# Row elimination on the Gram matrix in place of Gram-Schmidt, and unpadded keys for the first four maxima of each block

## The chip, the cores and the metric

The kernel runs on one core of a Trainium2 chip. The metric is the device time of one execution in microseconds. The engines are TensorE (PE, with its weight loads as PEld), VectorE (DVE), ScalarE (ACT), GpSimd (POOL) and SyncE (SP). Each takes its own instructions in program order and waits on semaphores. ACTq and SPq in rows are the two engines' queues as they issue transfers.

## The reference

Input x is [2, 512, 144] in float32, with a condition vector of 144 for each of the two batch rows. Three transformer layers and a rotation follow:

```python
x = layer0(x, c)   # attention with 16 heads of 9, then a mixture of 4 experts, top 2
x = layer1(x, c)   # attention with layer-normed q and k, then an MLP of 576
x = layer2(x, c)   # attention, then an MLP of 576
# the rotation
U, _ = jnp.linalg.qr(P)              # P is [144, 64]
R = expm(A)                          # A skew, 64 x 64, from silu(c) @ W.T + b
z = jnp.einsum('btn,nd->btd', x, U)
z_rot = jnp.einsum('btd,bde->bte', z, R)
x_rot = x + jnp.einsum('btd,nd->btn', z_rot - z, U)
```

U has the signs that a Householder QR gives its columns, so an orthonormal basis of P alone does not suffice.

## The kernel before, in words

**Attention.** There are six blocks (3 layers x 2 batch rows). In a block the 16 heads stand in 4 groups of 4; a group has 16 steps, a block 64, the program 384. A step n runs on PE: `max_scores` for the next group (one query tile of 128 against 512 keys, into one of three banks `m_bank`), `scores(n)` (128 keys against 512 queries, into one of two banks `s_bank`), every fourth step `pv` (4 products into `o_bank`, two records each in the trace). ACT takes the exponential of `s_bank` (L687), DVE the row maximum of `m_bank` (`take_max`, L849). The first two steps of a group have two `max_scores` each. `max_turn` and `place_max` put the maxima into `q_t` before the group's scores begin.

**Keys.** `k_t` holds the keys of 4 heads stacked in 4 strips of 32 rows. `k_pad` holds each head's strip alone with zeros in the other rows, so that a product of full height with the stacked queries gives one head's scores. ACT issues four transfers `k_pad<-k_t` for each group (`pad_keys`, L674); for the first group of a block it does so right after the exponential of the last step before that group's maxima begin. The maxima of the very first group read `q_t` and `k_t` in strips of 32 rows, without `k_pad` (L1289); all others wait for `pad_in` and read `k_pad` (L1292).

**Side stages.** The other stages (norms, qkv, projections, MLPs; `d_bank`) are woven into the steps by `SLOTS`, at places fixed by hand. None fall on the last 18 steps of a block.

**The solver.** U and R come from three chains of small steps that share the banks `m_bank` with the maxima: `V_CHAIN`, `QR_CHAIN` and `EXP_CHAIN`. `QR_CHAIN` has 135 parts: `p_load` (P transposed into `q_rows`, 64 x 144), 64 parts `mgs`, `unit_cols`, 64 parts `lu`, which find the Householder signs, and 5 that end it. Its first 16 parts run in the head of the program: one with each slot of the head's stages, then one after each pair of the 16 maxima of the first group. The others follow every 2.5 steps (`QR_PACE`). A part `mgs` j is: PE spreads row j over 64 partitions (L1478), DVE copies it (L1083), takes its square (L1084) and its product with all rows (L1087), a reciprocal (L1093), a factor (L1094) and subtracts (L1096). PE's next part waits for L1096 (`last[chain]`), and PE, in order, holds all that stands behind it. In the middle of a part DVE takes one waiting maximum (`fill`). The banks are used in turn by maxima and parts alike, so PE's third product after a part waits for the part's last instruction.

## Time and profile before

| | |
|---|---|
| runs (3) | 1034.75, 1039.34, 1040.19 us; median 1039.34 |
| profiled execution | 1034.67 us |
| its span, first to last instruction | 1032.5 us |
| PE, DVE, ACT, POOL busy | 777.3, 665.5, 383.6, 167.7 us |
| mean granted TensorE clock | 0.812 of full speed |

The span's 1032.5 us are what the trace shows; 2.2 us of the execution lie outside it. A busy time is a mean over stages whose limits differ, so the stages are read one by one. A granted clock of 0.50 is 1.2 GHz and one of 1.00 is 2.4 GHz; values between are means over both.

### The profile page before, as it was taken

The numbers are of one execution on the slowest core, as the hardware profiler recorded it, in microseconds if no ns is written. First come the engines' busy times: TensorE is split into PE (matmuls) and PEld (weight loads), VectorE is DVE, ScalarE is ACT, GpSimd is POOL, SyncE is SP. The second block draws the span as 40 slices with busy tenths as digits, with TensorE's granted clock in tenths as the row PEclk, the third lists the DMA queues.
The fourth block names the chain that finished last, engine by engine and source line by source line (L and its number), as shares of the span: only waits on it lengthen the run. The fifth ranks groups of instructions, "written<-read, shape, count | busy, mean of one in ns | idle before, by whom it ended". The sixth has DMA issues, their size and how long they took to land.

```text
span 1032.5 us, 11456 instructions
## 1 busy us (share of the span) xinstructions
PE 777.3 (75%) x3551; PEld 451.6 (44%) x3551; DVE 665.5 (64%) x2080; ACT 383.6 (37%) x682; POOL 167.7 (16%) x349
## 2 busy tenths in 40 slices
PE   5465788786898757878876787679788678898846
PEld 1232354333665433445644444346444354445425
DVE  4568877788435886784358678756578565675332
ACT  0220354242353333334424333324434336555511
POOL 6201002202130210023230000301100311003020
PEclk9955787897799757788987589797889789999856
DMA  2110001110022000001210000000000000100000
GB/s 78 49 31 0 24 22 30 38 27 1 11 58 62 0 1 22 10 11 46 59 30 1 10 11 11 27 13 1 11 11 11 27 14 5 26 11 1 6 6 11
DMA packets 22717, 21.26 MB, mean 21 GB/s; under 512 B 4831, under 2 KB 17015, under 8 KB 22658
## 3 DMA queue, kind: packets, MB, share of 16 engines
q1 hardware_dynamic: 18002, 14.22, 5.0%
q10 hardware_dynamic: 4656, 6.31, 2.6%
q8 instruction: 29, 0.48, 0.2%
q14 instruction: 30, 0.25, 0.1%
HBM read 13.62 MB, written 0.61 MB: 14 GB/s over the span
## 4 chain that ended last, share of the span: by engine, by line
PE 48%; DVE 39%; issue 5%; ACT 3%; POOL 2%; DMA 1%; ACTq 1%; DVEq 0%; SPq 0%; POOLq 0%
DVE row_max L849 11%; PE m_bank L1292 8%; PE o_bank L1314 7%; PE d_bank L1428 6%; PE s_bank L1275 6%; PE m_bank L1478 2%; DVE q_rows L1096 2%; PE d_bank L1375 2%; PE m_bank L1301 2%; PE d_bank L1419 2%; DVE h_tok L908 2%; DVE bc_sq L1084 1%; PE d_bank L1422 1%; PE d_bank L1420 1%; PE d_bank L1421 1%
## 5 line engine op out<-in xcount | busy, mean ns | idle before, releaser
L687 ACT ACTIVATE probs<-s_bank 128x512 f32<-128x512 f32 x384 | 222.7, 597 | 473.5 <-PE s_bank L1275 464.0
L849 DVE TENSOR_REDUCE row_max<-m_bank 128x1 fp32r<-128x512 f32 x384 | 255.7, 686 | 143.1 <-PE m_bank L1292 138.3
L1292 PE MATMUL m_bank<-k_pad,q_t 128*128 128x512 f32 x368 | 193.1, 545 | 85.1 <-DVE q_rows L1096 23.4
L1275 PE MATMUL s_bank<-q_t,k_pad 128*128 128x512 f32 x384 | 179.5, 472 | 3.6 <-ACT probs L687 2.8
L1292 PEld LDWEIGHTS m_bank<-k_pad,q_t 128*128 128x128 f32 x368 | 80.0, 225 | 167.9 <-issue 61.3
L1314 PE MATMUL o_bank<-probs,v_aug 128*32 128x512 f32 x768 | 124.8, 728 | 3.5 <-DVE o_tok L867 2.8
L1275 PEld LDWEIGHTS s_bank<-q_t,k_pad 128*128 128x128 f32 x384 | 87.0, 227 | 24.8 <-ACT probs L687 11.8
L1428 PE MATMUL d_bank<-w,g_act 128*128 128x144 f32 (+1 forms) x480 | 61.8, 287 | 8.7 <-issue 8.7
L1428 PEld LDWEIGHTS d_bank<-w,g_act 128*128 128x128 f32 (+1 forms) x480 | 59.5, 190 | 14.6 <-ACT g_act L755 13.1
L598 POOL TENSOR_TENSOR h_tok<-h_tok,mod 128x144 f32<-128x144 f32 x48 | 24.0, 500 | 255.5 <-DVE h_tok L908 255.5
L1478 PE MATMUL m_bank<-q_rows,ident 64*64 64x144 f32 x128 | 36.3, 373 | 18.9 <-DVE q_rows L1096 18.9
L601 POOL COPY h_tok<-o_tok 128x144 f32<-128x144 f32 x24 | 7.4, 306 | 241.4 <-DVE o_tok L867 203.9
L616 POOL TENSOR_TENSOR qs_tok<-qkv_tok,qs_tok 128x144 fp32r<-128x144 f32 x24 | 12.2, 506 | 209.7 <-ACT ks_tok L738 209.7
L1301 PE MATMUL m_bank<-ident_r,row_max 128*128 128x128 f32 x96 | 19.6, 338 | 34.5 <-DVE q_rows L1096 12.2
L755 ACT ACTIVATE g_act<-d_bank 128x512 f32<-128x512 f32 (+1 forms) x60 | 35.5, 596 | 26.1 <-PE d_bank L1422 26.1
L1301 PEld LDWEIGHTS m_bank<-ident_r,row_max 128*128 128x128 f32 x96 | 16.2, 239 | 59.0 <-issue 33.9
L1346 PE MATMUL d_bank<-ident,h_tok 128*128 128x128 f32 x80 | 27.1, 354 | 19.3 <-POOL h_tok L602 19.3
L1083 DVE COPY bc_row<-m_bank 64x144 f32<-64x144 f32 x64 | 18.9, 296 | 28.4 <-PE m_bank L1478 27.7
L1478 PE MATMUL m_bank<-lu,ident 64*64 64x64 f32 x128 | 22.9, 265 | 18.7 <-DVE lu L1118 16.0
L856 DVE SCALAR_TENSOR_TENSOR q_t<-m_bank,q_t 128x512 fp32r<-128x512 f32 x24 | 16.6, 691 | 30.2 <-PE m_bank L1301 30.2
L1314 PEld LDWEIGHTS o_bank<-probs,v_aug 128*32 128x32 f32 x768 | 16.3, 116 | 42.4 <-issue 36.3
L1419 PE MATMUL d_bank<-h_hi,ff_hi 128*128 128x512 f32 (+1 forms) x60 | 27.5, 458 | 9.8 <-ACT g_act L755 4.4
(222 smaller groups left out, 1238.7 us busy)
## 6 DMA issues: line engine op xcount, KB each, us to landing
...
```

The costliest lines, as they stand in the source:

```text
L598: link(pool.tensor_tensor(tile, tile, mv[:, first + 1, :], ALU.mult))
L687: act.activation(probs[:, n % PROBS, :], s_banks[n % S_BANKS][:, :], ACT.Exp, scale=HD ** -0.5)\
L755: act.activation(g_act[rows, f, :], bk[rows, :], ACT.Gelu_apprx_tanh).then_inc(drained, 1)
L849: dve.tensor_reduce(row_max[:, grp % 2, t, MAXROW + 32 * j:MAXROW + 32 * j + 1], bk[:, :], AX.X, ALU.max).then_inc(drained, 1)
L1275: pe.matmul(s_banks[n % S_BANKS][:, :], k_pad[:, grp % PADS, j, kt * P:(kt + 1) * P], q_t[:, par, g, :], start=True, stop=True).then_inc(s ...
L1292: ins = pe.matmul(bk[:, :], q_t[:, par, g, t * P:(t + 1) * P], k_pad[:, grp % PADS, j, :], start=True, stop=True)
L1301: ins = pe.matmul(bk[:, t * P:(t + 1) * P], row_max[:, grp % 2, t, :], ident_r[:, :], start=True, stop=True)
L1314: ins = pe.matmul(o_bank[32 * j:32 * j + 32, :], v_aug[:, par, kt, at:at + 32], probs[:, (GRP * quad + j) % PROBS, :], start=(kt == 0), st ...
L1346: pe.transpose(a_bank[:, cols], h_tok[:, t, 0:P], ident[:, :])
L1419: pe.matmul(bk[0:n, :], ff_hi[:, i, c], h_hi[:, :], start=True, stop=False)
L1428: return pe.matmul(bk[:, t % 2 * C:(t % 2 + 1) * C], g_act[0:k, f, t * P:(t + 1) * P], w2[0:k, i, f, :], start=(f == 0), stop=(f == FT))
L1478: ins = pe.matmul(bk[0:S, 0:src.shape[1]], ident[0:S, j:j + 1].to_broadcast([S, S]), src, start=True, stop=True)
```

## The change

It has three parts.

1. `mgs` becomes `elim`. The 64 x 64 product of P with itself is put beside the rows of P (`gram_rows`, 64 x 208, of which `q_rows` is now the right part). Eliminating below the diagonal in the left part applies to the right part what Gram-Schmidt would. The pivot and the factors are then single elements: a reciprocal, one factor, one update of width 207 down to 144. The result is less exact, so after `unit` two rounds of `turn`, `gram` and `fix` follow, which make the rows orthogonal again (transpose, Gram matrix, one product with a correcting matrix). `QR_CHAIN` goes from 135 to 141 parts at the same pace.
2. `lu` works on the columns from j on alone, the signs are stored negated, and the factor is a plain product of two columns.
3. The four maxima of query tile 0 in the first group of each block read `k_t` in strips, as those of the very first group do, and the wait for `pad_in` moves to the first maximum of tile 1.

```diff
-QR_CHAIN = [("p_load",)] + [("mgs", j) for j in range(S)] + [("unit_cols",)]
+FIXES = 2
+QR_CHAIN = [("p_load",)] + [("elim", j) for j in range(S)] + [("unit",)]
+QR_CHAIN += [(kind, i) for i in range(FIXES) for kind in ("turn", "gram", "fix")]
...
-        q_rows = sb("q_rows", [S, C])
+        gram_rows = sb("gram_rows", [S, S + C])
+        q_rows = gram_rows[:, S:S + C]
+        q_cols = sb("q_cols", [P, 2, S])
+        fix_by = sb("fix_by", [S, S])
-        bc_row = sb("bc_row", [S, C])
-        bc_sq = sb("bc_sq", [S, C])
...
+            link(pool.memset(half_upper[:, :], -1.0))
+            link(pool.affine_select(out=half_upper[:, :], in_=half_upper[:, :], compare_op=ALU.is_gt, fill=0.0,
+                                    base=0, pattern=[[1, S]], channel_multiplier=-1))
+            link(pool.affine_select(out=half_upper[:, :], in_=half_upper[:, :], compare_op=ALU.not_equal, fill=-0.5,
+                                    base=0, pattern=[[-1, S]], channel_multiplier=1))
...
-                    act.activation(q_rows[:, :], bk[0:S, 0:C], ACT.Copy).then_inc(drained, 1)
+                    act.activation(gram_rows[:, :], bk[0:S, 0:S + C], ACT.Copy).then_inc(drained, 1)
...
-                elif kind == "mgs":
+                elif kind == "elim":
                     j = step[1]
-                    row = bk[0:S, 0:C]
                     dve.wait_ge(s["solver_full"], full)
-                    link(dve.tensor_copy(bc_row[:, :], row))
-                    dve.tensor_tensor_reduce(out=bc_sq[:, :], in0=bc_row[:, :], in1=bc_row[:, :], scale=1.0, scalar=0.0,
-                                             op0=ALU.mult, op1=ALU.add, accum_out=s_small[:, 3:4])\
-                        .then_inc(s["dve_done"], 1)
-                    dve.tensor_tensor_reduce(out=bc_scr[0:S, :], in0=q_rows[:, :], in1=bc_row[:, :], scale=1.0,
-                                             scalar=0.0, op0=ALU.mult, op1=ALU.add, accum_out=s_small[:, 0:1])\
-                        .then_inc(s["dve_done"], 1)
-                    done[0] += 2
+                    dve.reciprocal(s_small[:, 1:2], bk[0:S, j:j + 1]).then_inc(s["dve_done"], 1)
+                    done[0] += 1
                     fill[0]()
                     dve.wait_ge(s["dve_done"], done[0])
-                    link(dve.reciprocal(s_small[:, 1:2], s_small[:, 3:4]))
-                    link(dve.tensor_scalar(s_small[:, 2:3], s_small[:, 0:1], s_small[:, 1:2], neg_after[:, j:j + 1],
-                                           ALU.mult, ALU.mult))
-                    drain(dve.scalar_tensor_tensor(out=q_rows[:, :], in0=bc_row[:, :], scalar=s_small[:, 2:3],
-                                                   in1=q_rows[:, :], op0=ALU.mult, op1=ALU.add))
-                elif kind == "unit_cols":
-                    link(dve.tensor_tensor_reduce(out=bc_scr[0:S, :], in0=q_rows[:, :], in1=q_rows[:, :], scale=1.0,
+                    link(dve.scalar_tensor_tensor(out=s_small[:, 2:3], in0=gram_rows[:, j:j + 1],
+                                                  scalar=s_small[:, 1:2], in1=neg_after[:, j:j + 1],
+                                                  op0=ALU.mult, op1=ALU.mult))
+                    right = gram_rows[:, j + 1:S + C]
+                    drain(dve.scalar_tensor_tensor(out=right, in0=bk[0:S, j + 1:S + C], scalar=s_small[:, 2:3],
+                                                   in1=right, op0=ALU.mult, op1=ALU.add))
+                elif kind == "unit":
+                    link(dve.tensor_tensor_reduce(out=bc_scr[0:S, :], in0=q_rows, in1=q_rows, scale=1.0,
                                                   scalar=0.0, op0=ALU.mult, op1=ALU.add,
                                                   accum_out=s_small[:, 0:1]))
                     rsqrt(s_small[:, 1:2], s_small[:, 0:1], s_small[:, 2:3])
-                    link(dve.tensor_scalar(q_rows[:, :], q_rows[:, :], s_small[:, 1:2], None, ALU.mult))
-                    dve.tensor_copy(lu[:, :], q_rows[:, 0:S]).then_inc(s["col_done"], 1)
+                    dve.tensor_scalar(q_rows, q_rows, s_small[:, 1:2], None, ALU.mult).then_inc(s["col_done"], 1)
+                    dve.wait_ge(s["col_done"], 1)
+                elif kind == "turn":
+                    dve.wait_ge(s["solver_full"], full)
+                    link(dve.tensor_copy(q_cols[:, 0, :], bk[:, 0:S]))
+                    drain(dve.tensor_copy(q_cols[0:CR, 1, :], bk[0:CR, S:2 * S]))
+                elif kind == "gram":
+                    dve.wait_ge(s["solver_full"], full)
+                    link(dve.tensor_tensor(fix_by[:, :], bk[0:S, 0:S], half_upper[:, :], ALU.mult))
+                    drain(dve.scalar_tensor_tensor(out=fix_by[:, :], in0=eye, scalar=1.5, in1=fix_by[:, :],
+                                                   op0=ALU.mult, op1=ALU.add))
+                elif kind == "fix":
+                    dve.wait_ge(s["solver_full"], full)
+                    drain(dve.tensor_copy(q_rows, bk[0:S, 0:C]))
+                    if step[1] == FIXES - 1:
+                        dve.tensor_copy(lu[:, :], q_rows[:, 0:S]).then_inc(s["col_done"], 1)
+                        dve.wait_ge(s["col_done"], 2)
                 elif kind == "lu":
                     j = step[1]
                     dve.wait_ge(s["solver_full"], full)
                     w = bk[0:S, j:j + 1]
-                    link(dve.tensor_scalar(s_sign[:, j:j + 1], w, 0.0, 2.0, ALU.is_ge, ALU.mult))
-                    dve.scalar_tensor_tensor(out=s_small[:, 0:1], in0=s_sign[:, j:j + 1], scalar=-1.0, in1=w,
-                                             op0=ALU.add, op1=ALU.add).then_inc(s["dve_done"], 1)
+                    link(dve.tensor_scalar(s_sign[:, j:j + 1], w, 0.0, -2.0, ALU.is_ge, ALU.mult))
+                    dve.scalar_tensor_tensor(out=s_small[:, 0:1], in0=s_sign[:, j:j + 1], scalar=1.0, in1=w,
+                                             op0=ALU.add, op1=ALU.subtract).then_inc(s["dve_done"], 1)
                     done[0] += 1
                     fill[0]()
                     dve.wait_ge(s["dve_done"], done[0])
                     link(dve.reciprocal(s_small[:, 1:2], s_small[:, 0:1]))
-                    link(dve.tensor_scalar(s_small[:, 2:3], lu[:, j:j + 1], s_small[:, 1:2], neg_after[:, j:j + 1],
-                                           ALU.mult, ALU.mult))
-                    drain(dve.scalar_tensor_tensor(out=lu[:, :], in0=bk[0:S, 0:S], scalar=s_small[:, 2:3],
-                                                   in1=lu[:, :], op0=ALU.mult, op1=ALU.add))
+                    link(dve.tensor_tensor(s_small[:, 2:3], lu[:, j:j + 1], s_small[:, 1:2], ALU.mult))
+                    drain(dve.scalar_tensor_tensor(out=lu[:, j:S], in0=bk[0:S, j:S], scalar=s_small[:, 2:3],
+                                                   in1=lu[:, j:S], op0=ALU.mult, op1=ALU.add))
...
-                if grp and t == 0 and j == 0:
+                if grp and (t, j) == (1 if grp % G == 0 else 0, 0):
                     pe.wait_ge(pad_in[grp % PADS], 16 * GRP * (grp // PADS + 1))
                 bk, _ = take(mring)
-                if grp == 0:
+                if grp == 0 or (grp % G == 0 and t == 0):
...
-                    pe.transpose(bk[0:S, 0:P], p_nat[:, :], ident[:, :])
-                    ins = pe.transpose(bk[0:S, P:C], p_nat_d[:, :], ident[0:CR, 0:CR])
-                elif kind in ("mgs", "lu"):
+                    pe.matmul(bk[0:S, 0:S], p_nat[:, :], p_nat[:, :], start=True, stop=False)
+                    pe.matmul(bk[0:S, 0:S], p_nat_d[:, :], p_nat_d[:, :], start=False, stop=True)
+                    pe.transpose(bk[0:S, S:S + P], p_nat[:, :], ident[:, :])
+                    ins = pe.transpose(bk[0:S, S + P:S + C], p_nat_d[:, :], ident[0:CR, 0:CR])
+                elif kind in ("elim", "lu"):
                     j = step[1]
-                    src = q_rows[:, :] if kind == "mgs" else lu[:, :]
+                    src = gram_rows[:, j:S + C] if kind == "elim" else lu[:, j:S]
                     if kind == "lu" and j == 0:
+                        pe.wait_ge(s["col_done"], 2)
+                    else:
+                        pe.wait_ge(*last[chain])
+                    ins = pe.matmul(bk[0:S, j:j + src.shape[1]], ident[0:S, j:j + 1].to_broadcast([S, S]), src,
+                                    start=True, stop=True)
+                elif kind == "turn":
+                    if step[1] == 0:
                         pe.wait_ge(s["col_done"], 1)
                     else:
                         pe.wait_ge(*last[chain])
-                    ins = pe.matmul(bk[0:S, 0:src.shape[1]], ident[0:S, j:j + 1].to_broadcast([S, S]), src,
-                                    start=True, stop=True)
+                    pe.transpose(bk[:, 0:S], q_rows[:, 0:P], ident[0:S, 0:S])
+                    ins = pe.transpose(bk[0:CR, S:2 * S], q_rows[:, P:C], ident[0:S, 0:S])
+                elif kind == "gram":
+                    pe.wait_ge(*last[chain])
+                    pe.matmul(bk[0:S, 0:S], q_cols[:, 0, :], q_cols[:, 0, :], start=True, stop=False)
+                    ins = pe.matmul(bk[0:S, 0:S], q_cols[0:CR, 1, :], q_cols[0:CR, 1, :], start=False, stop=True)
+                elif kind == "fix":
+                    pe.wait_ge(*last[chain])
+                    ins = pe.matmul(bk[0:S, 0:C], fix_by[:, :], q_rows, start=True, stop=True)
```

**PE, where the maxima of the third block's first group begin (its steps 48 to 50 of the block before).** In these rows `m_bank<-k_pad,q_t` and `m_bank<-k_t,q_t` are maxima, `s_bank` scores, `ident_r,row_max` is `max_turn`, and L1478 or L1497 is a part of the solver. Before:

```order
L1301 MATMUL m_bank<-ident_r,row_max 128x128 x4
L1478 MATMUL m_bank<-q_rows,ident 64x144
L1275 MATMUL s_bank<-q_t,k_pad 128x512
L1292 MATMUL m_bank<-k_pad,q_t 128x512 x2
L1275 MATMUL s_bank<-q_t,k_pad 128x512
L1478 MATMUL m_bank<-q_rows,ident 64x144
L1292 MATMUL m_bank<-k_pad,q_t 128x512 x2
L1275 MATMUL s_bank<-q_t,k_pad 128x512
L1292 MATMUL m_bank<-k_pad,q_t 128x512
L1275 MATMUL s_bank<-q_t,k_pad 128x512
```

The same place in the changed kernel:

```order
L1318 MATMUL m_bank<-ident_r,row_max 128x128 x4
L1497 MATMUL m_bank<-gram_rows,ident 64x149
L1292 MATMUL s_bank<-q_t,k_pad 128x512
L1306 MATMUL m_bank<-k_t,q_t 128x512 x2
L1292 MATMUL s_bank<-q_t,k_pad 128x512
L1497 MATMUL m_bank<-gram_rows,ident 64x148
L1306 MATMUL m_bank<-k_t,q_t 128x512 x2
L1292 MATMUL s_bank<-q_t,k_pad 128x512
L1309 MATMUL m_bank<-k_pad,q_t 128x512
L1292 MATMUL s_bank<-q_t,k_pad 128x512
```

No instruction has moved; the first reader of the new `k_pad` is now the ninth row in place of the fourth.

**DVE, one part of the solver in the head of the program.** Before:

```order
L1083 COPY bc_row<-m_bank 64x144
L1084 ISA bc_sq,s_small<-bc_row 64x144
L1084 ISA s_small 64x1
L1087 ISA bc_scr,s_small<-q_rows,bc_row 64x144
L1087 ISA s_small 64x1
L1093 RECIPROCAL s_small<-s_small 64x1
L1094 TENSOR_SCALAR s_small<-s_small,neg_after 64x1
L1096 SCALAR_TENSOR_TENSOR q_rows<-bc_row,s_small,q_rows 64x144
```

Two such parts in the changed kernel, with the two maxima between them:

```order
L1091 RECIPROCAL s_small<-m_bank 64x1
L1095 SCALAR_TENSOR_TENSOR s_small<-gram_rows,s_small,neg_after 64x1
L1099 SCALAR_TENSOR_TENSOR gram_rows<-m_bank,s_small,gram_rows 64x200
L858 TENSOR_REDUCE row_max<-m_bank 128x1 x2
L1091 RECIPROCAL s_small<-m_bank 64x1
L1095 SCALAR_TENSOR_TENSOR s_small<-gram_rows,s_small,neg_after 64x1
L1099 SCALAR_TENSOR_TENSOR gram_rows<-m_bank,s_small,gram_rows 64x199
```

Eight rows have become three, and the last one is wider.

**PE, where the first correcting round stands (around step 128).** `gram_rows` transposed is `turn`, `q_cols` is `gram`. In the changed kernel alone:

```order
L1504 MATMUL m_bank<-ident,gram_rows 128x64
L1505 MATMUL m_bank<-ident,gram_rows 16x64
L1292 MATMUL s_bank<-q_t,k_pad 128x512
L1331 MATMUL o_bank<-probs,v_aug 32x512 x4
L1318 MATMUL m_bank<-ident_r,row_max 128x128 x4
L1292 MATMUL s_bank<-q_t,k_pad 128x512
L1508 MATMUL m_bank<-q_cols 64x64
L1509 MATMUL m_bank<-q_cols 64x64
```

These rows stand where parts `lu` stood before; every later part `lu` comes 15 steps later.

## Rows read from the trace of the kernel before

**Rows 1.** The page: busy time of engines; chain that ended last, by engine.

```profile
PE 777.3 (75%) x3551; PEld 451.6 (44%) x3551; DVE 665.5 (64%) x2080; ACT 383.6 (37%) x682; POOL 167.7 (16%) x349
...
PE 48%; DVE 39%; issue 5%; ACT 3%; POOL 2%; DMA 1%; ACTq 1%; DVEq 0%; SPq 0%; POOLq 0%
```

**Rows 2.** Windows: us, PE, PEld, DVE, ACT, POOL busy, PEclk, DMA, GB/s.

```profile
64.00:90.00 26.00, 16.00 (x34) 6.88 (x35) 23.93 (x88) 0.00 (x0) 0.00 (x0) 0.50 0.13 31
90.00:166.00 76.00, 57.82 (x221) 29.53 (x220) 64.25 (x244) 28.43 (x55) 7.53 (x18) 0.72 0.06 16
...
415.00:845.00 430.00, 333.35 (x1634) 199.94 (x1634) 285.48 (x890) 162.32 (x279) 70.40 (x141) 0.82 0.07 18
```

**Rows 3.** PE's waits: us in total, times, longest us.

```profile
PE m_bank L1292 <- DVE q_rows L1096: 23.4, 15, 6.3
PE m_bank L1292 <- DMA k_pad<-k_t: 20.9, 5, 4.3
...
PE m_bank L1478 <- DVE q_rows L1096: 18.9, 20, 1.5
...
PE m_bank L1478 <- DVE lu L1118: 16.0, 9, 5.6
PE m_bank L1292 <- DVE lu L1118: 15.6, 18, 4.8
...
PE m_bank L1301 <- DVE q_rows L1096: 12.2, 6, 4.7
```

**Rows 4.** PE's waits from 90 to 415 us.

```profile
PE m_bank L1478 <- DVE q_rows L1096: 10.5, 11, 1.5
```

**Rows 5.** The chain from 60 to 130 us: start, us, what.

```profile
65.61 1.29 DVE row_max L849 x2
...
68.60 1.29 DVE row_max L849 x2
```

**Rows 6.** DVE's instructions by form: busy us, mean ns of one.

```profile
L1118 DVE SCALAR_TENSOR_TENSOR lu<-m_bank,s_small,lu 64x64 f32<-64x64 f32 x64 | 17.7, 276 | 2.2
L1094 DVE TENSOR_SCALAR s_small<-s_small,neg_after 64x1 f32<-64x1 f32 x64 | 17.0, 265 | 2.3
...
L1110 DVE SCALAR_TENSOR_TENSOR s_small<-s_sign,m_bank 64x1 f32<-64x1 f32 x64 | 9.4, 147 | 2.2
```

**Rows 7.** Instructions by form from 64 to 90 us, DVE, then PE.

```profile
L1096 DVE SCALAR_TENSOR_TENSOR q_rows<-bc_row,s_small,q_rows 64x144 f32<-64x144 f32 x9 | 3.2, 360 | 0.3
...
L1289 PE MATMUL m_bank<-k_t,q_t 32*128 32x512 f32 x16 | 10.5, 787 | 0.2 <-ACT k_t L721 0.2
```

**Rows 8.** Timeline of PE from 407 to 414 us, with DVE's L1096.

```profile
407.46 0.36 DVE L1096 SCALAR_TENSOR_TENSOR q_rows<-bc_row,s_small,q_rows 64x144 f32<-64x144 f32 x1
410.85 0.36 DVE L1096 SCALAR_TENSOR_TENSOR q_rows<-bc_row,s_small,q_rows 64x144 f32<-64x144 f32 x1
...
411.92 0.46 PE L1478 MATMUL m_bank<-q_rows,ident 64*64 64x144 f32 x2
...
412.87 0.40 PE L1292 MATMUL m_bank<-k_pad,q_t 128*128 128x512 f32 x1
...
413.43 1.06 PE L1314 MATMUL o_bank<-probs,v_aug 128*32 128x512 f32 x8
```

**Rows 9.** Timeline of PE at the first and the last block's `k_pad` wait.

```profile
195.71 1.19 PE L1292 MATMUL m_bank<-k_pad,q_t 128*128 128x512 f32 x2 [4.08 <-DMA k_pad<-k_t]
...
199.47 0.63 PE L1292 MATMUL m_bank<-k_pad,q_t 128*128 128x512 f32 x1
...
879.33 1.19 PE L1292 MATMUL m_bank<-k_pad,q_t 128*128 128x512 f32 x2 [4.29 <-DMA k_pad<-k_t]
...
882.03 0.63 PE L1292 MATMUL m_bank<-k_pad,q_t 128*128 128x512 f32 x1
```

**Rows 10.** Windows: 3 us behind the first of these waits.

```profile
198.00:201.00 3.00, 2.98 (x9) 1.70 (x13) 2.66 (x4) 0.62 (x2) 0.00 (x0) 0.50 0.01 1
```

**Rows 11.** Timeline of POOL in the head.

```profile
31.68 0.49 POOL L598 TENSOR_TENSOR h_tok<-h_tok,mod 128x144 f32<-128x144 f32 x1 [11.81 <-DVE h_tok L908]
```

5 lines of the change are left out of this document (3 added, 2 removed).

## The prediction

> **What bounds the kernel now.** I read the page first. PE is busy for 75% of the span and DVE for 64%, and the chain that ended last runs over PE for 48% and over DVE for 39% [rows 1]. So neither engine sets the time alone: the two take turns, and what counts is where PE stands still for DVE. The windows say where. From 64 to 90 us DVE is busy for 23.93 of 26.00 us and PE for 16.00; from 90 to 166 us it is 64.25 against 57.82 of 76.00; in the long stretch of parts `lu`, from 415 to 845 us, it has turned: DVE 285.48, PE 333.35 of 430.00 [rows 2]. Then PE's waits, longest sums first. The update that ends a part `mgs` (L1096) held PE 41 times, for 23.4 + 18.9 + 12.2 = 54.5 us. The end of a part `lu` (L1118) held it 27 times, 31.6 us. The transfers into `k_pad` held it 5 times, 20.9 us, once at each block's start but the first [rows 3]. The change touches these three and no others, so 107 us of standing PE is the most it can work on.
>
> **The new part `elim`, its own cost.** In the head the chain goes from one pair of maxima to the next in 68.60 - 65.61 = 2.99 us, of which the pair takes 1.29; a part `mgs` thus takes 1.70 us of DVE, gaps counted [rows 5]. The new part has three instructions. The reciprocal reads one PSUM column; the nearest row is L1110, also one element from PSUM, 147 ns. The factor has a scalar from memory and a second column. The update L1118 of 64 columns with such a scalar takes 276 ns [rows 6], L1096 with 144 columns 360 ns [rows 7]: 1.05 ns a column and 209 ns besides, so one column costs 210 ns; the ends are 147 (L1110, no scalar from memory) and 265 (L1094, two of them) [rows 6]. The wide update has 207 down to 144 columns, 176 on average: 209 + 1.05 x 176 = 394 ns. With three gaps of 40 ns the part takes 0.87 us at the start and 0.83 at the mean, 0.87 less than before.
>
> A rule speaks against the new form, because two of its three instructions read PSUM where one of eight did before. L1118 reads its first operand from PSUM and L1096 from SBUF, and one line with one intercept fits both [rows 6, 7]; I see no surcharge. The Trainium skill, VectorE: DVE Perf Modes, in the section on the TRN2 errata, puts a fixed 120 cycles on a PSUM source against 58 for SBUF at 0.96 GHz, an estimated 65 ns for each such read. By it the saving of a part would be 0.80 us and the sum below some 3 us smaller; the rows decide for me.
>
> **What of it reaches the end.** *Head, 8 pairs.* DVE would need 1.29 + 0.87 = 2.16 us a pair. PE is busy for 16.00 us over the 8 pairs, 2.0 each at half clock, and its product grows from 144 to some 200 columns, so it needs about 2.2 and becomes the equal of DVE. I take 2.4 us a pair: 8 x 0.6 = **5 us** (ends 3 and 6.6).
>
> *Woven parts, 90 to 415 us.* Here L1096 held PE 11 times before L1478 [rows 4], and the other two waits on it, 15 and 6 times, all lie in this stretch too [rows 3]: 32 waits, 46.1 us. If each shrank by the full 0.87 us it would be 28 us. But look at a stretch of plain attention at full clock: the ends of two parts lie 410.85 - 407.46 = 3.39 us apart, which is DVE working without a pause. PE needs in the same 2.5 steps 5 products of 0.40, 2.5/4 of the 8 records that take 1.06, and 0.46 for the part: 2.0 + 0.66 + 0.46 = 3.1 us [rows 8]. So there only 0.3 to 0.4 us of the 0.87 can be won before PE is the bound. Where norms stand beside the part the whole 0.87 is won. Between 32 x 0.4 = 13 and 28 I take **18 us**.
>
> *Parts `lu`.* The factor loses a scalar from memory (265 to about 150 ns) and the update narrows from 64 to a mean of 32 columns (33 ns): 0.15 us a part. 27 waits of rows 3 by 0.15 is **4 us** (ends 2 and 5). The narrower product on PE (lu) and the wider one (elim) cancel.
>
> *The `k_pad` wait.* It stands before the first maximum; now four maxima, two scores and a part go ahead of it. Those took PE from 195.71 to 199.47, 3.8 us, at the first boundary, and from 879.33 to 882.03, 2.7 us, at the last, against waits of 4.08 and 4.29 us [rows 9]. The transfer lands when it did before, since ACT issues it after the same exponential. What is gained is the smaller of both: 4 x 3.8 + 2.7 = 18 us, with the whole 4.2 at the middle three 19; **17** taken, because DVE must free the banks in that time. The strips of 32 rows cost no more per product: at half clock a strip takes 787 ns with its tail [rows 7], and a padded pair 1.19 us with one tail for both [rows 9]. Were each of the 20 strips 0.1 us dearer, 2 us would go; with that and a wait of a microsecond left at three boundaries the low end is 12.
>
> *The clock.* Behind the wait at 195 us the granted clock is 0.50, though it is 1.00 before; in the window of 198 to 201 us PE is busy for 2.98 of 3.00 us at it [rows 10]. I count two such windows behind each of the first four waits, 24 us of work at half clock. If the standing goes, up to half of that, 12 us, comes back; DVE would bound in part of it. I take **6 us** (ends 0 and 12). The Trainium skill, TensorE: Matmul & The Clock Gate, Part 1, says that a PE left idle falls to 1.2 GHz and that sustained work brings 2.4 GHz back; rows 10 agree with the fall.
>
> *What is added.* Six parts more. Each is a round PE, DVE, PE with one to two short products and 0.3 to 0.5 us of DVE (two updates of 64 columns without a scalar from memory, about 0.21 each, by L1118 less 65 ns). PE waits for each of them as for a part `lu`, 31.6/27 = 1.2 us where it waits at all. Behind the waiting product stand scores and maxima, and ACT waits for those. Taken at 0.7 us each: **4 us** lost (ends 0 and 8). The three new POOL instructions in the head lie ahead of a wait of 11.81 us of POOL for DVE [rows 11]; without that cover they would cost a microsecond. The Gram product in `p_load` and the wider ACT copy lie where PE and DVE wait for the first norm: nothing, or half a microsecond without that.
>
> **Sum.** -5 - 18 - 4 - 17 - 6 + 4 = -46 us against the profiled execution's 1034.67: **989 us**. That execution was at the lower edge of the runs shown (1034.75 to 1040.19, median 1039.34), so a median may stand up to 5 us higher; I leave the 989. All low ends at once give -3 - 13 - 2 - 12 - 0 + 8 = -22, 1013; all high ends -6.6 - 28 - 5 - 19 - 12 + 0 = -71, 964.
>
> **Rivals.**
> *A. Both parts carry as summed:* 989. Chance 0.55.
> *B. PE is the bound sooner than I think.* For it: the 3.1 us of PE in 3.39 [rows 8], and PE's larger sum in the last window of rows 2. Against it: 54.5 us of waits on L1096 [rows 3]. Then the woven parts give 8 in place of 18 and the clock nothing: 1034.7 - 5 - 8 - 3 - 15 + 6 = 1010. Chance 0.20.
> *C. The stalls feed the low clock.* For it: 0.50 from 64 to 90 us and 0.72 behind it, while DVE is full [rows 2]. If PE no longer pauses, it stays at 2.4 GHz, its own 3.1 us do not double, and the high ends of 28 and 12 us are reached or passed: 1034.7 - 6 - 28 - 5 - 19 - 15 + 2 = 964. Chance 0.15.
> *D. The wait is only moved and the new parts are not shorter in effect:* the first maximum of tile 1 waits for what the first of tile 0 waited for, and the next score waits for the exponential behind ACT's four issues. For it: landing time is the same. Against it: nothing of the work ahead depends on the transfer. With the parts gaining only in the head: within 0.5%, 1034 or so. Chance 0.04.
> *E. Slower.* PE with shorter bursts and more waits on six added round trips gets less of the full clock in the long stretch. There the granted clock is 0.82, so 0.36 of 430 us, 155 us, are at 1.2 GHz [rows 2]; work bound by PE takes twice the time at it. If the other terms give 46 us, a further 92 us of the stretch would have to fall to the low clock to cancel them; beyond a share of (155 + 92)/430 = 0.57 the kernel is slower; at 0.62 it would stand at 1045. Against it: the change shortens waits and lengthens none but the six. Chance 0.03.
> The last 0.03 lie between D and B.
>
> **How the numbers follow.** Measured times of this kernel differ by 0.5% among themselves, so a change below that can't be told from none. A, B and C are all faster by more: 0.90, and most of the rest between D and B, 0.93. Same: 0.04. Slower: 0.03. The range for 8 in 10 runs from C to B: 963 to 1013. A alone would be 978 to 1000.
>
> **What the profile after would show.** A part `elim` in the head takes 0.83 to 0.90 us of DVE and pairs of maxima lie 2.2 to 2.5 us apart. DVE's busy time falls by 64 x 0.87 + 9, less 3 for the new parts, to about 605 us, while PE's changes little but for the clock. Waits of PE on the update of `gram_rows` sum to 20 to 30 us in place of 54.5. The wait for `k_pad` is below 1 us at four boundaries and stands at the fifth maximum. The clock does not fall behind a boundary. The forecast is wrong if PE's waits move to other releasers with the same sum, if the wide update takes well above 0.4 us, or if a score at the boundary waits for ACT's issues.

## The result, and the profile after

The changed kernel takes 966.39 us (median of four executions, 958.46 to 969.33) against 1037.05 us (1034.19 to 1040.19) for the kernel before, measured beside it: a ratio of 0.9284 with an interval of 0.9238 to 0.9331. The forecast was 989 us with a range of 963 to 1013. The direction is right. The median lies inside the range, 3 us above its low end; by the ratio, taken on the execution that the forecast started from, the time is 0.9284 x 1034.67 = 960.6 us and below it. The gain was forecast at 46 us and measured at 71 by the medians, 74 by the ratio (0.0716 of 1034.67), and 75.8 by the spans of the two profiled executions, 1032.5 and 956.7.

The page of the changed kernel: its span, the busy time of each engine, and the chain that ended last by engine.

```profile
span 956.7 us, 11202 instructions
...
PE 763.2 (80%) x3571; PEld 441.8 (46%) x3571; DVE 601.3 (63%) x1770; ACT 381.8 (40%) x682; POOL 167.3 (17%) x352
...
PE 55%; DVE 33%; issue 5%; ACT 3%; POOL 2%; DMA 1%; ACTq 1%; SPq 0%; DVEq 0%; POOLq 0%
```

Against [rows 1] DVE lost 64.2 us of work, and PE lost 14.1 us although it now runs 20 records more: the same products ran more often at the high clock. The chain has moved from DVE to PE, 39% to 33% and 48% to 55%.

PE's waits after: us in total, times, longest.

```profile
PE m_bank L1497 <- DVE lu L1135: 15.2, 7, 5.5
PE m_bank L1309 <- DVE row_max L858: 14.0, 13, 3.8
...
PE m_bank L1309 <- DVE gram_rows L1099: 11.6, 6, 5.1
PE m_bank L1309 <- DVE lu L1135: 10.7, 10, 3.6
...
PE m_bank L1318 <- DVE gram_rows L1099: 7.9, 3, 5.0
...
PE m_bank L1497 <- DVE gram_rows L1099: 3.3, 9, 0.7
PE m_bank L1309 <- DMA k_pad<-k_t: 2.6, 3, 1.1
```

These answer to [rows 3]. The waits on the elimination's last instruction fell from 54.5 to 22.8 us (20 to 30 were forecast), those on `k_pad` from 20.9 to 2.6, those on `lu` from 31.6 to 25.9.

DVE's new instructions by form: busy us, mean ns of one, idle before. The means of the first two are raised by a few long ones (last section): their medians are 203 and 152 ns.

```profile
L1095 DVE SCALAR_TENSOR_TENSOR s_small<-gram_rows,s_small,neg_after 64x1 f32<-64x1 f32 x64 | 14.5, 226 | 1.2 <-DVE s_small L1091 0.3
L1134 DVE TENSOR_TENSOR s_small<-lu,s_small 64x1 f32<-64x1 f32 x64 | 11.9, 185 | 2.2
L1091 DVE RECIPROCAL s_small<-m_bank 64x1 f32<-64x1 f32 x64 | 10.0, 156 | 36.4 <-PE m_bank L1497 35.6
```

The chain in the head: start, us, what.

```profile
66.58 1.29 DVE row_max L858 x2
67.87 0.08 DVE s_small L1091
67.97 0.22 DVE s_small L1095
68.21 0.43 DVE gram_rows L1099
68.67 1.29 DVE row_max L858 x2
```

From pair to pair it is 68.67 - 66.58 = 2.09 us, where [rows 5] had 2.99. Of the reciprocal's 0.156 us only 0.08 lie on the chain: PE's product for the part is ready before the second maximum ends, and the reciprocal starts under it. Every pair in the head runs in this order, with DVE alone on the chain: PE was not the second bound that the prediction saw there.

Windows after: us, PE, PEld, DVE, ACT, POOL busy, PEclk, DMA, GB/s. The first stands at the same clock times as in [rows 2]; the work in it does not, since the kernel is further on. The second covers the nine groups that follow the head, from the first `place_max` to the tenth, the same stretch as 90.78 to 454.13 before. This is called the stretch from here on.

```profile
64.00:90.00 26.00, 22.54 (x50) 10.10 (x49) 21.55 (x62) 2.29 (x4) 0.00 (x0) 0.50 0.13 31
...
84.52:392.47 307.95, 256.20 (x1195) 143.61 (x1195) 214.55 (x641) 133.09 (x238) 53.03 (x101) 0.87 0.10 26
```

The same stretch before:

```profile
90.78:454.13 363.35, 279.00 (x1191) 156.41 (x1191) 263.96 (x906) 134.88 (x238) 54.27 (x101) 0.78 0.08 22
```

So 6.3 us of the 75.8 came in the head, 363.35 - 307.95 = 55.4 in this stretch, which holds 49 of the 64 parts and two boundaries (places where a block's first group begins), and 14.1 behind it, 11.9 of them in the three groups behind the other boundaries. Of the 55.4 us, 22.8 are PE's own busy time and 32.6 are time in which it stood. In the head and behind the stretch PE's busy time rose, by 4.2 and 4.5 us, which leaves the 14.1 of the page. In the whole kernel PE stood 61.7 us less and was busy 14.1 us less.

### The profile page after: what moved, and what is told of

The parts are those of the page before. It is cut to its first block, busy times and chain, and to the rows that moved or that the text cites. A ratio compares the mean times of both kernels' runs of the same rounds, so it can differ in the third digit from the quotient of the medians.

```text
span 956.7 us, 11202 instructions
## 1 busy us (share of the span) xinstructions
PE 763.2 (80%) x3571; PEld 441.8 (46%) x3571; DVE 601.3 (63%) x1770; ACT 381.8 (40%) x682; POOL 167.3 (17%) x352
## 4 chain that ended last, share of the span: by engine, by line
PE 55%; DVE 33%; issue 5%; ACT 3%; POOL 2%; DMA 1%; ACTq 1%; SPq 0%; DVEq 0%; POOLq 0%
DVE row_max L858 10%; PE m_bank L1309 9%; PE o_bank L1331 8%; PE s_bank L1292 7%; PE d_bank L1445 6%; PE m_bank L1497 3%; PE d_bank L1392 2%; PE m_bank L1318 2%; DVE h_tok L917 2%; PE d_bank L1436 2%; DVE gram_rows L1099 1%; PE d_bank L1437 1%; PE d_bank L1439 1%; PE d_bank L1438 1%; PE d_bank L1363 1%
## 5 line engine op out<-in xcount | busy, mean ns | idle before, releaser
L1309 PE MATMUL m_bank<-k_pad,q_t 128*128 128x512 f32 x348 | 177.6, 524 | 49.2 <-DVE row_max L858 14.0
L1292 PE MATMUL s_bank<-q_t,k_pad 128*128 128x512 f32 x384 | 176.7, 464 | 3.3 <-ACT probs L696 2.3
L1309 PEld LDWEIGHTS m_bank<-k_pad,q_t 128*128 128x128 f32 x348 | 72.6, 213 | 125.6 <-issue 37.1
L1331 PE MATMUL o_bank<-probs,v_aug 128*32 128x512 f32 x768 | 119.6, 699 | 4.1 <-DVE o_tok L876 3.4
L1292 PEld LDWEIGHTS s_bank<-q_t,k_pad 128*128 128x128 f32 x384 | 83.4, 218 | 25.4 <-ACT probs L696 12.9
L607 POOL TENSOR_TENSOR h_tok<-h_tok,mod 128x144 f32<-128x144 f32 x48 | 24.4, 507 | 241.0 <-DVE h_tok L917 241.0
L625 POOL TENSOR_TENSOR qs_tok<-qkv_tok,qs_tok 128x144 fp32r<-128x144 f32 x24 | 11.9, 495 | 189.4 <-ACT ks_tok L747 189.4
L1497 PE MATMUL m_bank<-gram_rows,ident 64*64 64x208 f32 (+42 forms) x128 | 40.3, 403 | 3.8 <-DVE gram_rows L1099 3.3
L865 DVE SCALAR_TENSOR_TENSOR q_t<-m_bank,q_t 128x512 fp32r<-128x512 f32 x24 | 16.6, 691 | 32.3 <-PE m_bank L1318 32.3
L1497 PE MATMUL m_bank<-lu,ident 64*64 64x64 f32 (+42 forms) x128 | 20.9, 244 | 15.9 <-DVE lu L1135 15.2
L1091 DVE RECIPROCAL s_small<-m_bank 64x1 f32<-64x1 f32 x64 | 10.0, 156 | 36.4 <-PE m_bank L1497 35.6
```

Of the source, the lines that this page charges most:

```text
L607: link(pool.tensor_tensor(tile, tile, mv[:, first + 1, :], ALU.mult))
L1292: pe.matmul(s_banks[n % S_BANKS][:, :], k_pad[:, grp % PADS, j, kt * P:(kt + 1) * P], q_t[:, par, g, :], start=True, stop=True).then_inc(s ...
L1309: ins = pe.matmul(bk[:, :], q_t[:, par, g, t * P:(t + 1) * P], k_pad[:, grp % PADS, j, :], start=True, stop=True)
L1331: ins = pe.matmul(o_bank[32 * j:32 * j + 32, :], v_aug[:, par, kt, at:at + 32], probs[:, (GRP * quad + j) % PROBS, :], start=(kt == 0), st ...
L1497: ins = pe.matmul(bk[0:S, j:j + src.shape[1]], ident[0:S, j:j + 1].to_broadcast([S, S]), src, start=True, stop=True)
```

## The experiments

Times are ratios to the kernel before, run beside it on the same chip, with their intervals; 0.01 is 10.4 us. The changed kernel stands at 0.9284. Most intervals are 0.006 to either side, so two of these kernels can be told apart only from some 8 us on. Single stretches of the same code differ by 3 us or more from kernel to kernel (last section). Each profile is of one execution, and the changed kernel's is the fastest of its four (958.46 us; the others took 964.42 to 969.33). "Group" is one of the 24 groups of 16 steps; its length is read from one start of `place_max` (L865 in the changed kernel) to the next.

**e1, the strips undone.** All keys of the maxima read padded after the first group, and the wait for `k_pad` stands where it was.

```diff
-                if grp and (t, j) == (1 if grp % G == 0 else 0, 0):
+                if grp and t == 0 and j == 0:
...
-                if grp == 0 or (grp % G == 0 and t == 0):
+                if grp == 0:
```

> The changed kernel, but with the maxima of each block's first group on k_pad as before, so elimination, fixes and the narrower lu alone. Theory 1: the gain of some 71 us is made of two parts, fewer waits and a TensorE that does less of its work at 1.2 GHz; the k_pad stall is worth 17 us by its waits and some 5 more by the clock behind it, so this kernel stands 17 to 25 us above the changed one, 983 to 991. Theory 2: the elimination brings its full 0.87 us at every one of 64 parts (56 us) and the strips only the rest: 10 us above the changed one, about 976.

Measured: 992.52 us, ratio 0.9534 (0.9473 to 0.9594). The stretch:

```profile
83.11:407.69 324.58, 267.79 (x1195) 149.15 (x1195) 215.26 (x640) 133.29 (x238) 52.98 (x101) 0.83 0.09 24
```

The head and the new parts alone bring 0.0466, 48 us, and 7.7 of these lie in the head. In the stretch DVE does 263.96 - 215.26 = 48.7 us less, and the stretch is 363.35 - 324.58 = 38.8 us shorter: 80% of what DVE was spared. Of the 38.8 us, 84.4 - 56.8 = 27.6 are time in which PE stood, and 279.00 - 267.79 = 11.2 are PE's own busy time, at a granted clock of 0.83 in place of 0.78. PE's waits that name the update fell by 20.5 of the 27.6, from 44.8 to 24.3; the rest is spread over waits that name other instructions of DVE and POOL.

**e2, the strips alone.** The kernel before with only part 3 of the change.

```diff
-                if grp and t == 0 and j == 0:
+                if grp and (t, j) == (1 if grp % G == 0 else 0, 0):
...
-                if grp == 0:
+                if grp == 0 or (grp % G == 0 and t == 0):
```

> The kernel before with the strips alone (part 3 of the change), the solver as it was. Theory 1: 1037 less 17 for the waits and up to 8 for the clock, 1012 to 1020, and behind each boundary the granted clock stays at 1.00. Theory 2: 1037 less 10, 1027. If the stall only moved (rival D), no change.

Measured: 1015.41 us, ratio 0.9778 (0.9701 to 0.9856), 23 us. The five groups behind a boundary shrank by 3.5, 4.9, 4.3, 4.3 and 2.5 us, 19.5 together; of the rest some may be noise. The granted clock over these groups was 0.86 to 0.91 (0.77 to 0.92 before), so it did not stay at 1.00, as theory 1 had it. The two halves multiply to 0.9534 x 0.9778 = 0.9322, within the intervals of the whole: they do not help or hinder each other by an amount that can be told.

**e3, the old `lu`.** The changed kernel with `lu` as before: full width on DVE and PE, the factor with two scalars from memory, the signs as they were. The core of the edit:

```diff
-                    link(dve.tensor_tensor(s_small[:, 2:3], lu[:, j:j + 1], s_small[:, 1:2], ALU.mult))
-                    drain(dve.scalar_tensor_tensor(out=lu[:, j:S], in0=bk[0:S, j:S], scalar=s_small[:, 2:3],
-                                                   in1=lu[:, j:S], op0=ALU.mult, op1=ALU.add))
+                    link(dve.tensor_scalar(s_small[:, 2:3], lu[:, j:j + 1], s_small[:, 1:2], neg_after[:, j:j + 1],
+                                           ALU.mult, ALU.mult))
+                    drain(dve.scalar_tensor_tensor(out=lu[:, :], in0=bk[0:S, 0:S], scalar=s_small[:, 2:3],
+                                                   in1=lu[:, :], op0=ALU.mult, op1=ALU.add))
```

> The changed kernel with the parts lu as before: all 64 columns, the factor with two scalars from memory, the signs not negated. Both theories, by the sum's term: 4 us above the changed kernel (2 to 5), about 970. If the lu stretch has a larger share of the unforeseen 25 us, it is 10 us or more above.

Measured: 965.13 us, ratio 0.928 (0.9221 to 0.9339). No difference that can be told. DVE was busy 7.1 us longer (608.4 for 601.3), but the interval of 6 us to either side is wider than the 4 us that part 2 was to give, so it neither shows nor excludes them.

**e4, more of PE, before.** The kernel before with two unread products ahead of each wait of a part `mgs`.

```diff
+DUMMIES = 2
...
+                    if kind == "mgs":
+                        for _ in range(DUMMIES):
+                            pe.matmul(bk[:, 0:P], ident[:, :], ident[:, :], start=True, stop=True)
```

> The kernel before, with two products of 128x128 that nothing reads put on TensorE ahead of its wait in each part mgs, DVE's work unchanged. They fill the wait and keep TensorE busy. Theory 1 (the half clock is part of the cost of the waits): fewer microseconds at 1.2 GHz from 90 to 415 us, and 5 to 15 us faster than before although DVE does the same and TensorE has 128 products more. Theory 2: no gain; where TensorE did not wait, each pair costs about 0.5 us, so 1037 to 1060.

Measured: 1061.37 us, ratio 1.0202 (1.0123 to 1.0281). PE's busy time rose by 33.1 us, to 810.4, and 21 of them came out at the end, so theory 1 is refuted: filling PE's pauses does not pay for itself. The stretch:

```profile
98.48:475.34 376.86, 297.82 (x1387) 181.36 (x1387) 263.48 (x905) 133.69 (x238) 54.10 (x101) 0.83 0.08 21
```

The granted clock there did rise, from 0.78 to 0.83, which fits rival C's picture, in which the stalls feed the low clock. But PE stood only 5.3 us less there, 79.0 for 84.4, and was busy 18.8 us more.

**e5 and e6, more of DVE, after.** The changed kernel with one and with two unread updates of 64 x 144 in each part `elim` (`EXTRA` is 1 and 2).

```diff
+                    for _ in range(EXTRA):
+                        link(dve.scalar_tensor_tensor(out=bc_scr[0:S, :], in0=q_rows, scalar=s_small[:, 2:3],
+                                                      in1=q_rows, op0=ALU.mult, op1=ALU.add))
```

> The changed kernel with one more update of 64x144 in each part elim, in DVE's chain ahead of the last one, that nothing reads: 0.40 us of DVE a part. Theory 1 (the prediction's cap): in plain attention TensorE needs 3.1 us in every 2.5 steps, so DVE's time there is free up to that; the first 0.40 us costs little, 0 to 8 us in all. Theory 2 (I mispriced TensorE: products of 512 columns start 0.23 us apart at full clock, not 0.40, so it needs about 2.1 us in 2.5 steps and DVE sets the pace before and after the change): the cost goes with DVE's time, 64 x 0.40 = 26 us less the parts in the MLP stretches, 18 to 24 us.

> The same with two such updates, 0.80 us a part, so that a part is nearly as long as mgs was (1.63 against 1.70 us). Theory 1: little for the first 0.40, most of the loss with the second: 15 to 25 us above the changed kernel and a curve that bends up. Theory 2: twice the cost of one, 36 to 46 us above, a straight line, and the kernel then stands near the one with the strips alone (ratio 0.978).

Measured: 982.54 us, ratio 0.9453 (0.9393 to 0.9513), and 1015.95 us, ratio 0.9769 (0.9676 to 0.9862). One such update in e5:

```profile
L1100 DVE SCALAR_TENSOR_TENSOR bc_scr<-gram_rows,s_small 64x144 f32<-64x144 f32 x64 | 27.1, 424 | 2.3
```

By the ratios 27.1 us of DVE cost 0.0169, 17.5 us; twice as many, 54 us, cost 0.0485, 50. With both of them DVE does nearly what it did in the kernel with strips alone (653.0 and 664.7 us busy), and the ratio is that of e2 as well, 0.9769 to 0.9778. So at neither of two widths between the new part and the old was DVE's time free. The second update costs about twice the first by the ratios, 33 us and 17.5; the intervals, 11 and 8 us to either side, leave it open whether they differ. The stretch with one and with two:

```profile
89.06:417.30 328.24, 263.66 (x1195) 146.66 (x1195) 236.87 (x689) 133.50 (x238) 53.26 (x101) 0.88 0.09 24
...
92.04:453.67 361.63, 282.32 (x1195) 154.55 (x1195) 255.65 (x739) 134.14 (x238) 53.27 (x101) 0.79 0.08 22
```

Against the changed kernel PE stands 12.8 and 27.6 us longer: this part is straight. What bends is PE's busy time for the same 1195 records, 7.5 us more, which one execution can differ from another by (as e3 and e7 show, in the part on the failed step), and 26.1 more, with the granted clock at 0.88 and 0.79. In e6 the third group took 42.3 us where it takes 25.6 in the changed kernel and 34.3 in the kernel before, and four long products of that group ran there at half rate.

```profile
188.63 1.64 PE L1352 MATMUL d_bank<-ada_a,c_wide_a 128*128 128x432 f32 x2
190.21 1.80 PE L1353 MATMUL d_bank<-ada_d,c_wide_d 17*128 17x432 f32 x2
```

The same two in the changed kernel:

```profile
155.42 0.89 PE L1348 MATMUL d_bank<-ada_a,c_wide_a 128*128 128x432 f32 x2
156.23 0.99 PE L1349 MATMUL d_bank<-ada_d,c_wide_d 17*128 17x432 f32 x2
```

**e10, more of PE, after.** The same two products as in e4 ahead of each wait of a part `elim`.

```diff
+                    if kind == "elim":
+                        for _ in range(2):
+                            pe.matmul(bk[:, 0:P], ident[:, :], ident[:, :], start=True, stop=True)
```

> The changed kernel with two unread products 128x128 ahead of each wait of a part elim, as e4_before_warm had them ahead of each wait of a part mgs, where they cost 20 us (ratio 1.020) for 33 us more of PE's busy time. T1 (before, DVE set the pace of the woven parts and PE had time to spare; now PE has less of it): they cost more than 20 us, 28 to 40, at 994 to 1006. T2 (PE was already the equal of DVE before, so little changed in its slack): they cost the 20 us again, 984 to 988.

Measured: 992.05 us, ratio 0.9521 (0.9464 to 0.9578), 0.0237 above the changed kernel: 25 us, between the two theories and inside neither, for 46 us more of PE's busy time. In groups 1 to 5, where 32 of the parts stand, the products cost 13.4 us here and 7.3 in e4. But e3 and e7, which have the same parts in these groups, take 3.2 and 3.8 us more there than the changed kernel's profile, and against them it is 10. In the whole stretch PE stood 5.5 us less with the products here and 5.3 less in e4, the same. The runs don't decide between the two theories.

**e7 and e8, fewer correcting rounds.** e7 leaves both rounds out, so U is less orthogonal than the reference's. e8 has one round, and a part every 3 steps in place of every 2.5.

```diff
-FIXES = 2
+FIXES = 0
```

```diff
-QR_PACE = 5
+QR_PACE = 6
-FIXES = 2
+FIXES = 1
```

> The changed kernel without the two rounds of turn, gram and fix, so that the basis stays less exactly orthogonal; QR_CHAIN is 135 parts as before. By the sum's term 4 us faster than the changed kernel (0 to 8). If the six round trips lie in cover, or TensorE has the slack that theory 2 gives it, 0 to 2.

> One round of correction in place of two, and a part of the chain every 3 steps in place of every 2.5, which just fits. The same parts are spread over 20 more percent of the steps, into the last block, where DVE has room. Theory 2: where DVE sets the pace a group of 16 steps has 5.3 parts in place of 6.4, but the stretch is that much longer, so DVE's sum only moves to where TensorE is the bound: 5 to 10 us faster than the changed kernel. Theory 1: TensorE is the bound in plain attention anyway, 0 to 3.

Measured: e7 964.15 us, ratio 0.9272 (0.9212 to 0.9332), so no cost of the six parts can be told; the interval doesn't exclude the 4 us of the forecast. e8 973.0 us, ratio 0.9364 (0.9303 to 0.9425), 8 us slower, where both theories had it equal or faster. Against the changed kernel its groups 10 and 11 take 6.5 and 5.5 us more, group 13 6.5 less, and the last four stretches 3.6, 10.4, 4.2 and 1.8 more: by these lengths the parts that a slower pace puts there cost more than those it takes away elsewhere.

**e9, denser parts.** A part every 2 steps, and the chain behind it begun earlier.

```diff
-QR_PACE = 5
-EXP_FROM = 141
+QR_PACE = 4
+EXP_FROM = 120
```

> The changed kernel with a part of the QR chain every 2 steps in place of every 2.5, and the chain behind it begun earlier. The work is the same; only its density moves from the last blocks to the first. T1 (DVE sets the pace wherever parts stand, each part costs its DVE time once): the groups 1 to 10 grow, those behind 14 shrink, and the sum stays within 4 us of the changed kernel's 966. T2 (PE is the bound between parts, and a part costs its round trip): where parts come oftener, each meets PE with less queued ahead, waits on L1099 grow by over 10 us, and the kernel is 8 us slower or more.

Measured: 992.35 us, ratio 0.9511 (0.9448 to 0.9573), 23 us slower. PE's waits:

```profile
PE m_bank L1309 <- DVE lu L1135: 34.0, 19, 6.4
```

against 10.7 us in the changed kernel. Groups 1 to 12 are longer than in the changed kernel, each of them, by 52 us together, and 15 to 20 shorter, by 19. T2's time fits and its place does not: the longest row on L1099 went from 11.6 to 9.0 us, and what grew were those on `lu`. That parts which come oftener than PE and DVE can take turns cost a wait each is one reading of it, not shown apart. The 2.5 steps lie between two worse paces.

**e11, e13 and e12, how many strips.** e11 has one correcting round and eight strips at a boundary, with the wait at the ninth maximum. e13 has two strips and the wait at the third. e12 has four in every group, and the waits of the changed kernel.

```diff
-                if grp and (t, j) == (1 if grp % G == 0 else 0, 0):
+                if grp and (t, j) == (2 if grp % G == 0 else 0, 0):
...
-                if grp == 0 or (grp % G == 0 and t == 0):
+                if grp == 0 or (grp % G == 0 and t < 2):
```

```diff
-                if grp and (t, j) == (1 if grp % G == 0 else 0, 0):
+                if grp and (t, j) == (0, 2 if grp % G == 0 else 0):
...
-                if grp == 0 or (grp % G == 0 and t == 0):
+                if grp == 0 or (grp % G == 0 and t == 0 and j < 2):
```

```diff
-                if grp == 0 or (grp % G == 0 and t == 0):
+                if grp == 0 or t == 0:
```

> The changed kernel with one correcting round in place of two, the first eight maxima of each block from k_t in strips in place of four, and the wait for k_pad at the ninth. T1 (the wait is 2.6 us in all by now, three times 0.9, and one round is worth 0 to 1 us): 963 to 966, no difference that can be measured. T2 (the four transfers still hold something back that the waits don't show, such as the clock behind the boundary): 955 to 960.

> The changed kernel with two strips at each boundary in place of four, and the wait for k_pad at the third maximum. The two other maxima, a score and the part stood ahead of the wait and took about 2 us. T1 (strips cost clock, and two cost less than four): the wait grows by 4 x 1.5 to 2 us and the clock gives back as much: 962 to 972. T2 (no clock hangs on them): the wait alone, 972 to 976.

> The changed kernel with the four maxima of tile 0 in strips of 32 rows in all 24 groups; it waits for k_pad where the changed kernel does (no wait goes away, since 18 of these groups found their keys there anyway). In e11_8_strip_maxima_one_fix four more strips at each boundary cost 3 to 5 us in the group, at unchanged waits of PE and with the clock down to 0.74. T1 (products of 32 rows go with the fall of the clock, wherever they stand): each of the 18 groups loses 1 to 4 us of time, with PE's busy time up by about as much: 985 to 1020. T2 (the fall at the boundary has another reason, such as what stood ahead of it): 963 to 972.

Measured at a boundary: none 0.9534 (e1), two 0.9425 (0.9361 to 0.9489, 979.2 us), four 0.9284, eight 0.9419 (0.9357 to 0.9481, 980.71 us). Both theories of e11 and both of e13 had the kernel faster than it was. The five groups behind a boundary together, in us:

| strips | length | PE busy | PE stood |
|---|---|---|---|
| none (e1) | 139.6 | 108.1 | 31.5 |
| two (e13) | 131.7 | 107.3 | 24.4 |
| four (changed kernel) | 114.8 | 100.9 | 14.0 |
| eight (e11) | 132.1 | 123.0 | 9.1 |

Up to four, strips take standing away and PE's busy time does not rise; T1 of e13, by which two fewer would give clock back, finds no support in them. With two the wait is back:

```profile
PE m_bank L1309 <- DMA k_pad<-k_t: 14.9, 5, 4.3
```

With eight it is gone and the time is lost all the same. Four of the five groups behind a boundary are 4.8, 3.3, 3.7 and 3.4 us longer than in the changed kernel, the fifth 2.0. The first of them, changed kernel:

```profile
162.77:184.43 21.66, 18.95 (x85) 8.19 (x85) 15.54 (x37) 9.55 (x17) 4.08 (x4) 0.92 0.14 31
```

and e11:

```profile
166.50:192.95 26.45, 24.21 (x85) 9.89 (x85) 15.78 (x38) 9.64 (x17) 4.06 (x4) 0.74 0.11 25
```

The same 85 records, the same work on DVE, ACT and POOL, and 5.3 us more of PE at a clock of 0.74. All five groups show it, with 22.1 us more of PE's busy time together. That e11 has one correcting round in place of two does not explain it: e7, with none and four strips, has 99.9 us there. So eight strips at a boundary come with the loss of the high clock; why is not shown. e12 asks whether they do so where no boundary is. It took 976.85 us, ratio 0.9409 (0.936 to 0.9458), less than its theory T1 had said and more than T2. Nor did each of the 18 groups lose, as T1 had it: some are up to 5 us longer and some as much as 3 us shorter. PE's busy time rose from 763.2 to 794.1 us with no instruction more; this sets the slowest of e12's four executions beside the fastest of the changed kernel's, and the ratios differ by 13 us. One place shows it, 3.1 us after the second `place_max` behind the head's in both. PE in the changed kernel, behind a wait of 0.85 us:

```profile
140.33 1.10 PE L1309 MATMUL m_bank<-k_pad,q_t 128*128 128x512 f32 x2 [0.85 <-DVE row_max L858]
141.27 0.40 PE L1292 MATMUL s_bank<-q_t,k_pad 128*128 128x512 f32 x1
...
142.52 0.40 PE L1292 MATMUL s_bank<-q_t,k_pad 128*128 128x512 f32 x1
142.84 1.06 PE L1331 MATMUL o_bank<-probs,v_aug 128*32 128x512 f32 x8
```

and in e12, behind the same wait, with strips in place of the padded keys:

```profile
143.26 1.39 PE L1306 MATMUL m_bank<-k_t,q_t 32*128 32x512 f32 x2 [0.85 <-DVE row_max L858]
144.58 0.80 PE L1292 MATMUL s_bank<-q_t,k_pad 128*128 128x512 f32 x1
...
145.81 0.63 PE L1292 MATMUL s_bank<-q_t,k_pad 128*128 128x512 f32 x1
146.37 1.94 PE L1331 MATMUL o_bank<-probs,v_aug 128*32 128x512 f32 x8
```

Scores of 0.40 us take 0.80, and the eight short products 1.94 in place of 1.06. The strips are no dearer by themselves, as the first boundary of the changed kernel shows:

```profile
163.31 0.70 PE L1306 MATMUL m_bank<-k_t,q_t 32*128 32x512 f32 x2
...
165.13 0.50 PE L1306 MATMUL m_bank<-k_t,q_t 32*128 32x512 f32 x2 [0.69 <-DVE gram_rows L1099]
...
167.07 0.68 PE L1309 MATMUL m_bank<-k_pad,q_t 128*128 128x512 f32 x1 [1.02 <-DMA k_pad<-k_t]
167.55 0.63 PE L1292 MATMUL s_bank<-q_t,k_pad 128*128 128x512 f32 x1
168.11 1.94 PE L1331 MATMUL o_bank<-probs,v_aug 128*32 128x512 f32 x8
```

The four strips run at full clock, two in 0.70 us and two in 0.50, and the fall comes behind them. Four at a boundary are the best number of the four tried.

None of the versions beats the changed kernel by an amount that can be told; e3 and e7 equal it.

## Why the prediction was wrong in size

**The step that failed: TensorE's need in the woven parts.** The prediction put 18 us on them (13 to 28), because "PE needs in the same 2.5 steps 5 products of 0.40, 2.5/4 of the 8 records that take 1.06, and 0.46 for the part: 2.0 + 0.66 + 0.46 = 3.1 us", so that of 0.87 us only 0.3 to 0.4 could be won. It added durations of products that overlap. The timeline of the changed kernel shows five steps of plain attention with two parts, and a third part with its wait:

```profile
172.63 0.47 PE L1497 MATMUL m_bank<-gram_rows,ident 64*64 64x172 f32 x2 [0.29 <-DVE gram_rows L1099]
...
173.37 0.39 PE L1292 MATMUL s_bank<-q_t,k_pad 128*128 128x512 f32 x1
173.60 0.39 PE L1309 MATMUL m_bank<-k_pad,q_t 128*128 128x512 f32 x1
173.83 0.40 PE L1292 MATMUL s_bank<-q_t,k_pad 128*128 128x512 f32 x1
...
178.16 0.47 PE L1497 MATMUL m_bank<-gram_rows,ident 64*64 64x170 f32 x2 [0.71 <-DVE gram_rows L1099]
```

The products stand 0.23 us apart and are shown as 0.39 or 0.40 long. In five steps and two parts PE is taken for 178.16 - 172.63 - 0.71 = 4.8 us, 2.4 us per part, and it still waits for DVE at the end. One set of the eight `o_bank` records falls in these five steps, where 1.25 would on average; with 0.1 us for that it is 2.5, not 3.1. The prediction read 3.1 in 3.39 and saw 0.3 us of room; there was 0.9, as much as the part's whole saving. Rival B rested on the same 3.1.

What the runs showed in its place: in e1 the stretch gave 38.8 us, 27.6 of standing and 11.2 of PE's busy time, for the 18 of the sum. The 27.6 are the 28 of the prediction's high end. For the 11.2 the sum had no term at all: its 6 us of clock belonged to the `k_pad` waits alone. Of the 28 us between the forecast's 46 and the ratio's 74 the two together are 21. The first part is the surer. In e3 and e7, which have the same parts `elim`, PE stands 51.0 and 52.5 us in the stretch, against 51.7 in the changed kernel, but is busy 260.2 and 263.9 us against 256.2: several us of PE's busy time come and go from one execution to the next.

**Which waits count.** The sum went over 32 waits that name the update as releaser. In e1 these gave 20.5 of the 27.6 us; 7.1 came from waits that name something else. DVE works in order, so a part that ends sooner also lets the next maximum free its bank sooner; this would explain the 7.1 and is not shown apart.

**The head.** Right in mechanism, small in size: 5 us forecast, 6.3 measured, 7.7 in e1. The part takes 0.80 us on the chain (0.87 forecast), since the reciprocal is half covered. PE was said to become the equal of DVE at 2.2 us a pair; pairs stand 2.09 apart, set by DVE. It is the same error at half clock: a strip there is shown as 0.79 us long and two as 1.19 together [rows 7], so they start 0.40 apart, and a busy time counts the tail behind the last of them.

**The new part's own cost.** Reciprocal 156 ns (147 taken); factor 226 in the mean, with a median of 203 (210 taken, ends 147 and 265); the wide update 0.43 us on the chain in the head (0.42 by the line of the prediction). The prediction's line, with one intercept for SBUF and PSUM, stood: DVE's busy time came to 601.3 us for a forecast of about 605. The rule of the Trainium skill, VectorE: DVE Perf Modes, section on the TRN2 errata, on a dearer PSUM source, would by an estimate have made each of the two instructions 65 ns longer. The wide update shows none of it: with 144 columns and its first operand in PSUM it takes 359 ns, where L1096 took 360 from SBUF. The reciprocal of one element takes 156 ns from PSUM (L1091) and 147 from SBUF (L1133 in a part `lu`): 9 ns, not 65.

**Parts `lu`.** Forecast 4 us; e3 can't tell it from nothing. The factor takes 185 ns in the mean with a median of 152, where about 150 were taken. The waits on `lu` fell from 31.6 to 25.9 us.

**The strips and the clock.** 17 us for the wait and 6 for the clock were forecast, 23 together; e2 measures 23 alone, e1 against the whole 26. By the pages, PE stood 18.7 us less with the strips and was busy 13.6 less (e1 against the changed kernel), or 12.2 and 9.5 (the kernel before against e2), so the split is roughly right too, as far as one execution of each shows. The wait is 1.0, 0.5 and 1.1 us at three boundaries and nothing at two, where under 1 us at four was forecast. The strips cost no more per product, as forecast. That the clock would not fall behind a boundary was wrong: behind the four strips of the first one the eight short products take 1.94 us, not 1.06. In the 6 us from the first padded product of each boundary on, the granted clock was 0.50 four times and then 0.73 in the kernel before; in the changed kernel it is 0.72, 0.61, 0.51, 0.76 and 1.00. So it is still below full speed at four of the five.

**The correcting rounds.** Forecast 4 us lost; e7 stands 1 us or less below the changed kernel, and its interval leaves room for the 4. None of PE's waits in the changed kernel names an instruction of a round; where the prediction had 0.7 us for each of the six, PE stood once at a round's first transpose, 1.6 us, for a row maximum.

**Rival C** forecast 964, and it comes nearest: its 28 us for the woven parts are the 27.6 of standing in e1, and its 12 for the clock lie beside the 11.2 there. Its picture holds only in part. PE did not stop pausing and the clock did not stay at 2.4 GHz: in e1 PE still stands 56.8 us in the stretch, at a granted clock of 0.83. In e6, where PE stands longer again, the clock is 0.79; e4 raises it to 0.83 but pays more for it than it gives. The larger part of the gain, 61.7 of 75.8 us, is time in which PE no longer stands. How much of PE's 14.1 us of busy time the shorter waits brought, and how much is chance of one execution, the runs do not part.
